# A decoder layer with eight experts: expert weights split and kept in a ring of three, three-part products, and attention with four value products at a time

## The reference

```python
x = layernorm(x + self_attention(x))        # 16 heads of 16, one k and v head
x = layernorm(x + cross_attention(x, ctx))  # 32 query heads of 8, 8 k and v heads
base_y = (silu(x @ bg[:, :512]) * (x @ bg[:, 512:])) @ base_down
probs = softmax(x @ gate_w)                 # 8 experts
w, idx = top_k(probs, 2); w = w / w.sum(-1)
out = sum over the two chosen experts of w * ((silu(x @ g_e) * (x @ u_e)) @ down_e)
x = layernorm(x + base_y + out)
```

## Time and profile before

| | us |
|---|---|
| median of three runs | 732.81 (731.70 to 733.79) |
| the profiled execution | 725.34 |
| its span | 723.5 |
| last `c_ln` starts, end of attention | 369.43 |
| window taken for the experts' opening (router, base tiles) | 370.10 to 441.80 |
| window taken for the sorted tiles | 441.80 to 676.85 |
| window taken for the last base tiles, shares, norm, stores | 676.85 to 723.50 |
| PE busy over the span | 660.0 (91%) |
| DVE, ACT, POOL busy | 383.3, 309.7, 135.3 |

### The profile page before, as it was taken

The page is one execution under the profiler, slowest core; times in us unless marked ns, Lnnn a source line. Parts: engine busy times, 40 slices in busy tenths (PEclk is TensorE's granted clock), DMA queues, the critical chain, the costliest instruction groups (busy, mean ns, idle before and its releaser), DMA issues. The chain is left out here.

```text
span 723.5 us, 10370 instructions
## 1 busy us (share of the span) xinstructions
PE 660.0 (91%) x3039; PEld 391.4 (54%) x3067; DVE 383.3 (53%) x884; ACT 309.7 (43%) x661; POOL 135.3 (19%) x155
## 2 busy tenths in 40 slices
PE   2778999999989999998679899999999999999991
PEld 2445555555545554543266566666666666666660
DVE  3568788898877888887625621111221211111286
ACT  2346666666656666665542112222222222222115
POOL 2011111111011111111000200233333333332100
PEclk9999999999999999999998999999999999999996
DMA  6100000000000000000049800011111111111343
GB/s 181 29 23 23 18 6 22 23 24 24 23 24 8 14 22 15 15 15 2 0 156 388 304 7 0 30 50 39 41 50 39 43 38 44 40 43 38 104 129 116
DMA packets 33073, 40.01 MB, mean 55 GB/s; under 512 B 5404, under 2 KB 28447, under 8 KB 33024
## 3 DMA queue, kind: packets, MB, share of 16 engines
q1 hardware_dynamic: 29280, 30.10, 12.8%
q0 software_dynamic: 3744, 9.31, 4.1%
HBM read 31.01 MB, written 9.31 MB: 56 GB/s over the span
## 5 line engine op out<-in xcount | busy, mean ns | idle before, releaser
L1299 PE MATMUL inner<-up,sortedT 128*128 x312 | 146.7, 592 | 0.0
L1162 DVE TENSOR_TENSOR hidden<-silu,inner 128x512 f32<-128x512 f32 x55 | 37.8, 686 | 170.8 <-PE inner L1299 170.1
L1039 ACT ACTIVATE silu<-inner 128x512 f32<-128x512 f32 x55 | 32.8, 597 | 191.6 <-PE inner L1299 191.6
L438 ACT ACTIVATE prob<-scores 128x1024 f32<-128x1024 f32 x96 | 98.3, 1026 | 11.5 <-PE scores L785 7.4
L565 DVE TENSOR_REDUCE max_c<-scores 128x8 f32<-128x1024 f32 x64 | 78.0, 1219 | 6.9 <-PE scores L848 5.8
L1299 PEld LDWEIGHTS inner<-up,sortedT 128*128 128x128 f32 x312 | 56.2, 190 | 39.4 <-issue 37.3
L1322 PE MATMUL y<-down,hT 128*128 x312 | 73.8, 379 | 0.0
L1015 POOL DMA_INDIRECT chosen_y<-y_rows,to_row x39 | 39.6, 1015 | 179.4 <-DVE y_rows L1173 175.5
L872 PE MATMUL sums<-prob,v_c 128*32 128x512 f32 x256 | 63.7, 621 | 0.0
L1299 PE MATMUL inner<-base_up,router_xT 128*128 128x512 f32 x128 | 61.4, 606 | 0.0
L1322 PEld LDWEIGHTS y<-down,hT 128*128 128x128 f32 x312 | 56.4, 190 | 7.0 <-issue 1.0
(11 more groups left out here) (187 smaller groups left out, 1052.2 us busy)
## 6 DMA issues: line engine op xcount, KB each, us to landing
up<-in_exp_gu SPq DMA_DIRECT2D x8, 1024.0 KB, 13.3
down<-in_exp_down SPq DMA_DIRECT2D x8, 512.0 KB, 12.2
up<-chosen_y SPq DMA_DIRECT2D x8, 512.0 KB, 8.3
xT_in<-in_xT SPq DMA_DIRECT2D x16, 128.0 KB, 2.2
x_in<-in_x SPq DMA_DIRECT2D x16, 128.0 KB, 2.2
x<-stream SPq DMA_DIRECT2D x1, 2048.0 KB, 10.0
ctxT_in<-in_ctxT SPq DMA_DIRECT2D x16, 96.0 KB, 2.3
out<-stream SPq DMA_DIRECT2D x2, 768.0 KB, 3.7
```

Source lines behind the costliest of these rows:

```text
L438: act.activation(prob[:, m, :], scores[:, n, :], ACT.Exp, scale=scale).then_inc(sem[exped], 1)
L1039: act.activation(silu[q % 2][:], inner[:, q % 2, 0, :], ACT.Silu).then_inc(sem["silu_set"], 1)
L1162: dve.tensor_tensor(hidden[q % 2][:], silu[q % 2][:], inner[:, q % 2, 1, :], ALU.mult).then_inc(sem["hidden_set"], 1)
L1299: mm = pe.matmul(inner[:, q % 2, h, :], tokens(q, k), w, start=(k == 0), stop=(k == 1))
```

## The change

The diff is long and does these things.

**Attention.** The hardware loop is written out. `c_sum` runs four products at once in two groups that add up in one bank, `s_sum` four at once; the sums of a stage now fill one bank instead of two, so `s_read`, `c_read`, `s_out`, `c_out`, `s_den` and `c_den` run once per sequence instead of twice. The ring of sums has one bank, that of `misc` three. The order tables are rewritten.

**New work inside the attention.** In each step SP loads half of an expert (768 KB), ACT writes its high half as f32r (`w_high`, two casts of 128x768), DVE the rest (`w_low`, three subtractions of 128x512), and SP stores both to DRAM (`store_w`, two times 768 KB). POOL splits the base weights once. Each finished tile is stored by SP (`store_x2`), transposed on PE (`x2_turn`), copied by ACT, and multiplied by the router's weights (`x2_logit`).

**Experts.** Gate and up products are three f32r products each (high by high, high by low, low by high) instead of one f32 product. The base tiles are taken in groups of four with the weights as the stationary side, so that the hidden rows come out transposed; their down products stay f32. The down products of the sorted tiles are three-part too, with the split of the turned rows and of the hidden rows on ACT and DVE. Eight base tiles come before the 39 sorted ones and eight behind. Weights lie in a ring of three experts (3 MB each): SP loads the next when the tiles of an old one are done, and POOL reads for each job from a table how many experts must have landed, waits for that, and signals `go`, for which PE waits.

```diff
-    ("s_den", 1, 1), ("s_out", 1, 1), ("c_max", 1, 0), ("s_rows", 0, 3), ("s_proj", 0, 1),
...
+    ("w_low", 2, 0), ("s_den", 0, 1), ("s_out", 0, 1), ("c_max", 1, 0), ("s_rows", 0, 3), ("s_proj", 0, 1), ("c_max", 2, 0),
...
+    ("load_xT", 0, 4), ("load_ctx", 0, 2), ("load_base", 0, 2), ("load_x", 0, 2), ("store_w", 0, 0), ("load_w", 0, 3),
+    ("store_x2", 0, -2),
...
-    return Ring(2, score), Ring(4, prob), Ring(2, summed), Ring(2, misc)
...
+    return Ring(2, score), Ring(4, prob), Ring(1, summed), Ring(3, misc)
...
+            def load_w(seq, unit):
+
+                wait(sp, sem["w_low"], seq.back(2), 3)
+                sp.dma_start(raw_w[seq.odd][:], expert_w[seq.off]).then_inc(w_loaded[seq.odd], 16)
+
+            def store_w(seq, unit):
+                wait(sp, sem["w_low"], seq, 3)
+                for part in range(2):
+                    at = PIECES * (2 * part + seq.odd)
+                    sp.dma_start(split[seq.off // 2, at:at + PIECES].rearrange("c p n -> p c n"),
+                                 f32(halves[seq.odd][:, part, :]).rearrange("p (c n) -> p c n", n=PIECE)).then_inc(split_stored[seq.odd], 16)
...
+            def w_high(seq, unit):
+
+                p, n = seq.odd, HALF // 2
+                wait_loaded(act, w_loaded, seq)
+                if unit == 0 and seq.off >= 2:
+                    wait_loaded(act, split_stored, seq.back(2), 2)
+                act.copy(halves[p][:, 0, n * unit:n * unit + n], raw_w[p][:, n * unit:n * unit + n]).then_inc(sem["w_high"], 1)
...
+            def c_sum(seq, a):
+
+                p, n = seq.odd, sum_ring.slot("c_sum", 0, seq)
+                wait(pe, sem["c_exp"], seq, 4, 2 * a + 2)
+                wait(pe, sem["ctx_v_set"], seq)
+                if a == 0:
+                    sum_ring.wait_free(pe, sem, "c_sum", 0, seq)
+                for j in range(4):
+                    m, v = prob_ring.slot("c_exp", 2 * a + j // 2, seq), j % 2
+                    mm = pe.matmul(sums[32 * j:32 * j + 32, n, :], v_c[p][:, P * a + 32 * j:P * a + 32 * j + 32],
+                                   prob[:, m, 512 * v:512 * v + 512], start=(a == 0), stop=(a == 1))
                 mm.then_inc(sem["c_summed"], 1)
...
+            for e in range(RING, EXPERTS):
+                done = sp.value_load(free_after[0:1, e - RING:e - RING + 1], min_val=FIRST_OUTS, max_val=FIRST_OUTS + SORTED)
+                sp.wait_ge(sem["y_full"], done)
+                load(e)
+                ready(e)
...
+            def go(j):
+
+                if j == 0:
+                    pool.wait_ge(sem["tile_set"], 1)
+                needed = pool.value_load(tile_ready[0:1, j:j + 1], min_val=1, max_val=EXPERTS)
+                pool.wait_ge(sem["weights_ready"], needed)
+                pool.sem_inc(sem["go"], 1)
...
             for j in range(SORTED):
                 if j + AHEAD < SORTED:
                     gather(j + AHEAD)
+                if j + 2 < SORTED:
+                    go(j + 2)
                 scatter(j)
...
+            def half(j, h):
+
+                u = use_of("sorted", j)
+                into = inner[:, u % 2, h, :]
                 if h == 0:
+                    pe.wait_ge(sem["turned_hi"], j + 1)
+                    if j == 0:
+                        pe.wait_ge(sem["tile_set"], 1)
+                    slot_of[j] = pe.value_load(tile_slot[0:1, j:j + 1], min_val=0, max_val=RING - 1)
+                    pe.wait_ge(sem["go"], j + 1)
+                free_inner(u, h)
+
+                def w(part, k):
+                    return weights[:, bass.ds(slot_of[j], 1), part, k, INNER * h:INNER * h + INNER].squeeze(1)
+
+                for k in range(2):
+                    pe.matmul(into, sT_hi[j % 2][:, k, :], w(0, k), start=(k == 0), stop=False)
+                    pe.matmul(into, sT_hi[j % 2][:, k, :], w(1, k), start=False, stop=False)
+                if h == 0:
+                    pe.wait_ge(sem["turned_lo"], j + 1)
+                for k in range(2):
+                    mm = pe.matmul(into, sT_lo[j % 2][:, k, :], w(0, k), start=False, stop=(k == 1))
+                mm.then_inc(sem["up_full" if h else "gate_full"], 1)
...
+            base_chunk(0, 0)
+            base_chunk(0, 1)
+            rank_tokens()
...
+            base_outer(0)
+            find_rows()
+            for c in range(1, CHUNKS):
+                base_chunk(1, c)
+            turn_rows(0)
+            turn_rows(1)
+            base_outer(1)
```

More of the change, by code:

```diff
@@ L967, in reach, with f32, y_bank @@
                 eng.wait_ge(s, v)
-        def sorted_before(q):
-            return sum(kind == "sorted" for kind, _ in jobs[:q])
-        def base_before(q):
-            return sum(kind == "base" for kind, _ in jobs[:q])
+        def f32(ap):
+            return ap.bitcast(F32)
+        def y_bank(o):
+            kind, n = outs[o]
+            return hiddenT[:, 0:2, :].rearrange("p a b -> p (a b)") if kind == "base" and n % 2 else y[:, 0:D]
         block = scope.enter_context(nc.Block())
@@ new lines, in _ @@
+            group_low(1)
+            multiply(2)
+            place_picks()
+            multiply(3)
+            hot_lanes()
+            multiply(4)
+            take(0)
+            take(1)
+            hot_slots()
+            take(2)
+            take(3)
+            multiply(5)
+            tile_experts()
+            multiply(6)
+            slot_rows()
+            multiply(7)
+            turn_rows(0)
+            turn_rows(1)
+            for o in range(TILES, FIRST_OUTS):
+                take(o)
@@ new lines, in _ @@
+            multiply(use_of("sorted", 0))
+            for j in range(SORTED):
+                if j:
+                    take(outs.index(("sorted", j - 1)))
+                if j == SORTED - 2:
+                    group_low(GROUPS_FIRST)
+                if j == SORTED - 1:
+                    group_low(GROUPS_FIRST + 1)
+                turn(j)
+                multiply(use_of("sorted", j) + 1)
+                if j + 2 < SORTED:
+                    turn_rows(j + 2)
+            take(outs.index(("sorted", SORTED - 1)))
@@ L1307, in turn_hidden @@
+            def turn_hidden(j):
+                pe.wait_ge(sem["hidden_set"], use_of("sorted", j) + 1)
+                reach(pe, sem["hT_lo"], j)
+                if j == 0:
+                    pe.wait_ge(sem["y_read"], FIRST_OUTS)
+                for c in range(CHUNKS):
+                    mm = pe.transpose(hiddenT[:, c, :], hidden[j % 2][:, P * c:P * c + P], ident[:])
                 mm.then_inc(sem["hT_full"], 1)
@@ L1342, in constants @@
+            for c in range(1, CHUNKS):
+                base_chunk(GROUPS_FIRST, c)
+            for c in range(CHUNKS):
+                base_chunk(GROUPS_FIRST + 1, c)
+            base_outer(GROUPS_FIRST)
+            base_outer(GROUPS_FIRST + 1)
 def constants():
```

664 lines of the change are left out of this document (402 added, 262 removed).

## The result

The changed kernel takes 698.41 us (692.76 to 700.74) against 732.25: 0.952 of the time before, 95% interval 0.947 to 0.958. It is faster, but by 34 us and not by the 60 that were forecast, and it lies outside the range of 645 to 694. The profiled execution took 698.20 us with a span of 696.4, so the whole miss can be read from its trace. The mean granted clock is 0.930; before it was 0.978.

A forecast was written before the change was run, and what follows sets the result against it. PE bounded the attention before; afterwards a loop through SP's queue would. Attention, opening, sorted tiles and end, 365 + 55 + 197 + 48 = 665 us, plus 1.84 is 667, times 1.0103 is 673; range 645 to 694.

The forecast's parts named there:

- what bounds the attention: Attention step: a loop through SP, ACT, PE and DVE, behind SP's load of `xT_in`, sets about 20.2 us.
- the landing: Attention: 768 + 128 + 128 KB must land before `xT_in` is there, 4.9 us, between 2.2 and 5.8.
- rival D: Attention: PE's clock falls in its pauses, at most 1.7 us in each of 12 steps, total 694; chance 0.06.
- A: The forecast itself: SP's list holds the attention step at 20.2 us, the gain comes from the experts; chance 0.49.
- rival C: Sorted tiles: a late `go`, gather or weight reload holds the job, at 5.5 us total 693; chance 0.14.
- The job itself: Sorted tiles: one job takes 5.0 us, 39 of them 195, the stage 197.
- The scale: Whole kernel: the summed 667 us times 1.0103, the earlier runs' median relative to the profiled execution, gives 673.
- Opening and end: Experts: the opening takes 55 us, between 44 and 64; the end 48, between 44 and 53.
- 5 us for the routing constants: Opening: DVE waits for the routing constants in front of the first low part, +5 us.
- B: Attention: SP's loop does not bind, DVE decides at 18.8 us a step, total 656; chance 0.27.

## Why the prediction was wrong, step by step

**Right: what bounds the attention.** The queue, not PE and not DVE, holds the step. Every link named is in the trace, and three experiments each open one link and free it. The numbers at full clock: from `w_low` to `s_res` 219.71 - 210.67 = 9.04 us, forecast 8.3; from there to the next `w_low` 231.33 - 219.71 = 11.62, forecast 11.8.

**Mis-sized: the landing.** From the start of `w_low` to the split I had 0.68 + 4.9. In the changed kernel it is 233.47 - 227.27 = 6.20. The landing itself, 4.6 from its issue at 228.85, was good (4.9 was forecast); the two DMAs that SP must issue first take 0.9 us, and I had left SP's issues at nothing. At full clock the same stretch is 216.79 - 210.67 = 6.12, 0.54 more than forecast; the other links come out even within 0.2. That makes up the 0.46 us between 20.66 and 20.2, 5 us over ten steps.

**The step that failed: the clock, rival D at 0.06.** The sum has no term for it. I argued that PE's pauses would be split up by the maxima and exponentials. But the forecast itself had all of ACT and DVE held by one load, so that they could not feed PE either, and the pause is one piece of 2.89 us. From `w_low` to `s_res` the loop grows from 9.04 to 9.79 us and behind it from 11.62 to 13.02: 2.2 us in that step. Ten steps, from the first `c_ln` at 103.98 to the eleventh at 325.80, average 22.18 us, 1.5 more than at full clock: 15 of the 24 us that the attention is over. D's price of 1.7 was near and its chance was not; A and D were not alternatives, the one caused the other. The rule of the Trainium skill that the prediction cites with D ("TensorE: Matmul & The Clock Gate", Part 1) agrees with these rows in direction: adding work to PE in the pause restored the full rate.

**The second miss: rival C, at 0.14, came in part.** The job itself is 5.0 us as worked out. The late gathers were in C's list, and cost 7.6 us: 198.98 - 191.39 in the pair of experiments. They show as waits of PE before the transposes of the gathered rows, not before line 1551's products, where the prediction looked for C. I had weighed the weights' own rate, which is ample, and not what 3 MB in one go do to a small gather beside it.

**The scale.** 1.0103 was taken as a property of the program; it was the luck of one profiled execution: runs of the kernel before lie between 724.66 and 736.07 us, 0.8% either side of the middle. Such a range belonged in the sum. As it was, the scale hid some 7 us of the miss.

**Opening and end** were 3.7 us shorter and 0.9 longer than worked out, within their bounds, the opening in part by luck: of its 5 us for the routing constants, loading them earlier gave back 0.6 at the first sorted product. B, the loop that does not bind, is what one digit in SP's list makes true: its step was put at 18.8, 18.14 was measured, and 656 in total against 650.71.

## What to carry to other kernels

When a change puts large transfers on a queue, read what small load stands behind them in the same list, who reads it, and what stands behind that reader on its engine: here 768 + 128 KB between a wait and a load of 128 KB cost 48 us through four engines, while the same bytes 10 us ahead of the load, or behind it, cost nearly nothing. When a bound moves from PE to a wait, look at the distances of the products behind the wait: here they nearly doubled behind a pause of 2.9 us (0.21 us, against 0.12 with the pause filled), and the price was that of the wait and the clock together. Work taken off the busiest engine pays only if nothing else is about as long, which 98% busy does not show: look for the chain that runs beside the very place from which the work is taken.

## What the runs showed of the hardware

- Three useless products in PE's pause made the kernel faster: granted clock 0.92 to 1.00 over four steps, spans 696.4 to 684.9 us.
- A gather of 128 rows lands in 2.7 to 4.1 us, median 2.8, with no reload of weights beside it, and in up to 7.6 with loads of 3 MB beside it.
- A DVE operation on 128x1 elements with an operand pair in SBUF took 0.96 us instead of 0.15 while POOL worked on SBUF tensors, and ended with POOL's instruction, and so did the one of 0.88. The Trainium skill, in "SBUF — State Buffer" ("SBUF: two separate sides"), says that the two engines share one pair of ports by an exclusive lock for a whole instruction, which a DVE operation with two inputs in SBUF contends for against a GpSimd operation that reads SBUF, and that the loser is fully blocked; these rows agree.
